# Cross-attention scores computed head by head in sixteen 32x32 places of the array, in plain fp32

## The reference, cut to what matters

```python
Q, K, V = x@Wq.T + bq, ctx@Wk.T + bk, ctx@Wv.T + bv      # 16 heads of 32
scores = einsum('bhqd,bhkd->bhqk', Q, K) / sqrt(32)
scores = where(scores <= softplus(raw_thresholds), -1e9, scores)
x = x + (softmax(scores) @ V -> 512) @ Wo.T + bo         # Q from layernorm(x)
```

## Time and profile before

| | |
|---|---|
| median of 3 runs | 1723.44 us |
| the profiled execution's own time | 1722.73 us |
| its span, first to last instruction | 1720.9 us |
| PE / PEld busy | 96% / 82% |
| DVE / ACT / POOL busy | 63% / 49% / 27% |
| granted TensorE clock, mean | 0.987 of full speed |

### The profile page before, as it was taken

One profiled execution on the slowest core, in us unless ns is written; L12 is line 12 of the kernel. 1 busy time (PEld: TensorE's weight loads), 2 busy tenths in 40 slices (PEclk: granted clock), 3 DMA queues, 4 the chain that ended last, 5 costly groups with the idle time before them and its releaser, 6 DMA issues.

```text
span 1720.9 us, 29176 instructions
## 1 busy us (share of the span) xinstructions
PE 1649.3 (96%) x10832; PEld 1402.7 (82%) x10832; DVE 1087.0 (63%) x2138; ACT 851.2 (49%) x1195; POOL 471.8 (27%) x357
## 2 busy tenths in 40 slices
PE   7999999999998899999998999999989999999997
PEld 6888889889887688788887887887877888888886
DVE  6554454554556767653337676635457989999995
ACT  4444444344444333344335233534416787878873
POOL 1443443444343344300004443300021121211311
PEclk9999999999999899999999999999999999999999
DMA  5011101110111300023224001224342443626612
GB/s 195 26 38 39 37 24 37 37 37 24 61 49 48 113 1 1 25 86 98 91 93 142 1 1 35 88 88 146 133 163 71 172 159 93 246 74 244 215 48 67
DMA packets 35977, 144.00 MB, mean 84 GB/s; under 512 B 4992, under 2 KB 5504, under 8 KB 28672
## 3 DMA queue, kind: packets, MB, share of 16 engines
q1 hardware_dynamic: 30736, 130.98, 21.7%
q0 software_dynamic: 5168, 12.06, 3.5%
HBM read 222.72 MB, written 12.85 MB: 137 GB/s over the span
## 4 chain that ended last, share of the span: by engine, by line
PE 56%; DVE 6%; DMA 2%; issue 1%; ACT 1%; SPq 0%; POOL 0%; DVEq 0%; POOLq 0%; ACTq 0%
PE bank L88 35%; PE bank L1608 9%; PE bank L2083 7%; PE bank L1505 2%; PE bank L2089 2%; PE bank L1592 1%; DVE e_w L2010 1%; DVE rc L1253 1%; DVE rs L1253 1%; DMA A<-xh_d,token 1%; DMA out<-acc_d 0%; PE bank L1517 0%; PE bank L1627 0%; DVE r_xh L1230 0%; DVE r_wg L1239 0%
## 5 line engine op out<-in xcount | busy, mean ns | idle before, releaser
L2010 DVE TENSOR_TENSOR e_w<-e_raw,e_w 128x2048 fp32r<-128x2048 f32 x134 | 302.4, 2284 | 20.3 <-ACT e_w L1892 19.8
L1892 ACT ACTIVATE e_w<-e_raw 128x2048 fp32r<-128x2048 f32 x134 | 256.6, 1918 | 38.4 <-PE bank L2083 19.2
L88 PE MATMUL bank<-e_w,e_xT 128*128 128x512 f32 x1104 | 272.1, 396 | 0.0
L88 PEld LDWEIGHTS bank<-e_w,e_xT 128*128 128x128 f32 x1104 | 204.3, 188 | 42.5
L88 PE MATMUL bank<-wv,ctx 128*128 128x512 f32 x768 | 190.8, 397 | 6.9 <-DVE kT L669 6.9
L88 PE MATMUL bank<-ctx,wk 128*128 128x258 f32 x1536 | 193.3, 285 | 2.1 <-issue 2.1
L88 PE MATMUL bank<-x2T,fw 128*128 128x512 f32 x768 | 190.4, 398 | 4.7 <-DVE fw L1314 4.7
L88 PEld LDWEIGHTS bank<-ctx,wk 128*128 128x128 f32 x1536 | 186.9, 190 | 4.0 <-issue 2.9
L1608 PE MATMUL bank<-fw,hh 128*128 128x512 f32 x768 | 186.1, 391 | 2.7 <-DVE hh L1432 2.7
L88 PEld LDWEIGHTS bank<-x2T,fw 128*128 128x128 f32 x768 | 145.2, 191 | 35.9 <-issue 5.0
L1608 PEld LDWEIGHTS bank<-fw,hh 128*128 128x128 f32 x768 | 143.9, 188 | 34.6 <-issue 2.2
(11 more groups left out here) (253 smaller groups left out, 2674.4 us busy)
## 6 DMA issues: line engine op xcount, KB each, us to landing
e_raw<-in_we SPq DMA_DIRECT2D x138, 1024.0 KB, 5.6
fraw<-in_wf SPq DMA_DIRECT2D x64, 512.0 KB, 3.5
ctxraw<-in_ctx SPq DMA_DIRECT2D x32, 514.0 KB, 3.5
wraw<-in_wa SPq DMA_DIRECT2D x20, 512.0 KB, 4.4
X<-in_x SPq DMA_DIRECT2D x4, 512.0 KB, 7.0
acc_d<-X SPq DMA_DIRECT2D x8, 256.0 KB, 4.5
xh_d<-A SPq DMA_DIRECT2D x8, 256.0 KB, 3.7
out<-acc_d SPq DMA_DIRECT2D x4, 512.0 KB, 5.9
```

What stands on the lines that cost most here:

```text
L88: last = nc.tensor.matmul(out, lhs(t, a), rhs(t, b), start=start and n == 0, stop=n == len(steps) - 1)
L1892: nc.scalar.activation(w[pos][:, 0, :, :], raw[pos][:, :, :], ACT.Copy).then_inc(m["w_hi"], 1)
L2010: nc.vector.tensor_tensor(w[pos][:, 1, :, :], raw[pos][:, :, :], r(w[pos][:, 0, :, :]), ALU.subtract).then_inc(m["w_lo"], 1)
```

## The change

- Queries and keys stay plain fp32: qT and kT have one half, the low halves of queries (eight VectorE instructions) and keys (four a batch) go, and the later steps wait for ScalarE's copy (`q_ok`, `k_ok`). GpSimd copies the batch's queries into qb (128 x 128) in place of qbd (128 x 1024).
- `score` becomes 16 plain fp32 products of 32 rows by 32 columns: head group g takes rows 32g to 32g+31, chunk c takes columns 32c to 32c+31, and the four g write four banks (4, 5, 2, 3). It stands as one piece ahead of the second half of V, and what it waits for is asked for before the last three products of the first half.
- All four thresholds follow each other; `turn(b-1)` stands behind the second half of V (and behind `project`); `attend` comes one batch later, between the second and third chunk of K, for batch b-2. `heads`, `bias_heads`, `project_lo` and `add_x` move with it: `add_x` from the body of k = 1 to the head of the body of k = 2.
- ScalarE copies both halves of V before `turned(b-1)`. In batch 31 it does the exponentials ahead of `turned(30)`; there `attend(30)` is done after the loop.
- The last row's product has plast as weights and the identity as moving operand; the constants own_q and same_head go, a block of ones comes.

TensorE in the third batch of the first tile: before, the scores stand in two pieces and `attend` at the end.

```diff
 S_BANK = (4, 5, 2, 3)
-        qT = sb("qT", [P, 2, DC, TOK], F32R)
+        qT = sb("qT", [P, DC, TOK])
-            kT = sbi("kT", [P, 2, DC, SKE], F32R)
+            kT = sbi("kT", [P, DC, SK])
@@ gpsimd
-                    def spread_q(b):
+                    def own_queries(b):
+                        nc.gpsimd.tensor_tensor(qb[:, :, :], qT[:, :, bass.ds(b * S, S)], ones[:, :].unsqueeze(1).broadcast_to([P, DC, S]),
+                                                ALU.mult).then_inc(qb_ok, 1)
@@ scalar
-                                nc.scalar.activation(kT[:, 0, dc, :], bank[K_BANK[dc]][:, 0:SKE], ACT.Identity, bias=col("bk", dc)).then_inc(k_hi, 1)
-                                if dc == 1 and k == 1 and not first:
+                                nc.scalar.activation(kT[:, dc, :], bank[K_BANK[dc]][:, 0:SK], ACT.Identity, bias=col("bk", dc)).then_inc(k_ok, 1)
+                                if dc == 3 and k == 1 and not first:
                                     heads_hi(it - 1)
...
-                            if not begin:
-                                turned(b - 1)
                             act.wait_ge(v_ps, 2 * b + 2)
                             nc.scalar.activation(v[k % 2][:, 1, :], bank[1][:, :], ACT.Copy).then_inc(v_ok, 1)
-                            exps(b)
+                            if last and k == BPT - 1:
+                                exps(b)
+                                turned(b - 1)
+                            else:
+                                if not begin:
+                                    turned(b - 1)
+                                exps(b)
@@ vector
-                            for dc in range(DC):
-                                dve.wait_ge(k_hi, DC * b + dc + 1)
-                                nc.vector.scalar_tensor_tensor(kT[:, 1, dc, :], ...
+                            if k == 2 and not first:
+                                add_x(it - 1)
+                            if not (first and k < 2):
+                                heads((k - 2) % BPT, b - 2)
                             if k == 1 and not first:
-                                add_x(it - 1)
+                                bias_heads(it - 1)
+                                project_lo(it - 1)
...
+                            threshold(b)
+                            softmax_terms(b)
...
                             weigh(b)
                             reciprocal(b)
-                            if not begin:
-                                heads((k - 1) % BPT, b - 1)
-                            if k == 0 and not first:
-                                bias_heads(it - 1)
@@ tensor
-                    def score(b, cs, begin):
...
+                    def score_waits(b, begin):
+                        pe.wait_ge(k_ok, DC * b + DC)
+                        pe.wait_ge(qb_ok, b + 1)
+                        if not begin:
+                            pe.wait_ge(u_ok, DC * b)
+                    def score():
+                        for g in range(HPC):
+                            rows = slice(g * XD, (g + 1) * XD)
+                            for c in range(DC):
+                                last = nc.tensor.matmul(bank[S_BANK[g]][c * S:(c + 1) * S, 0:SK], qb[rows, c, :], kT[rows, c, :], start=True, stop=True)
+                        last.then_inc(s_ps, 1)
...
+                                if dc == 1 and not (first and k < 2):
+                                    if not (first and k == 2):
+                                        pe.wait_ge(oT_ok, b - 2)
+                                    attend((k - 2) % BPT, b - 2, it if k == 2 and not first else None)
+                            pe.wait_ge(k_ok, DC * b + 1)
+                            for c in range(DC):
+                                if c == DC - 1:
+                                    score_waits(b, begin)
...
+                            score()
+                            pe.wait_ge(k_ok, DC * b + 2)
+                            products(nc, bank[1][:, :], range(DC), lambda c, h: ctx[k % 2][:, h, c, P:2 * P],
+                                     lambda c, h: wv[:, h, c, :]).then_inc(v_ps, 1)
                             if k == 1 and not first:
                                 project(it - 1)
                             if not begin:
-                                pe.wait_ge(k_lo, DC * b + DC)
                                 turn(b - 1)
-                            score(b, (0, 1), begin)
-                            value(1)
-                            score(b, (2, 3), begin)
```

More of the change, by code:

```diff
@@ L42 @@
 K_BANK = (0, 1, 4, 5)
+S_BANK = (4, 5, 2, 3)
 LATE_AT = 4
@@ L776, in turn @@
                         pe.wait_ge(plast_ok, b + 1)
-                        nc.tensor.matmul(bank[6][:, 0:P], same_head[:, :], plast[:, :, :].rearrange("p c n -> p (c n)"),
+                        if not (isinstance(b, int) and b == 0):
+                            pe.wait_ge(olast_ok, b)
+                        nc.tensor.matmul(bank[6][:, 0:P], plast[:, :, :].rearrange("p g n -> p (g n)"), ident[:, :],
                                          start=True, stop=True).then_inc(spread_ps, 1)
@@ L820, in body @@
                                          lambda c, h: ctx[k % 2][:, h, c, :]).then_inc(k_ps, 1)
-                            def value(kt):
-                                pe.wait_ge(k_lo, DC * b + 1 + kt)
-                                products(nc, bank[kt][:, :], range(DC), lambda c, h: ctx[k % 2][:, h, c, kt * P:(kt + 1) * P],
-                                         lambda c, h: wv[:, h, c, :]).then_inc(v_ps, 1)
-                            value(0)
+                                if dc == 1 and first and k == 1:
+                                    pe.wait_ge(u_ok, 2)
+                                if dc == 1 and not (first and k < 2):
[6 more added lines that the diff above has]
+                                    score_waits(b, begin)
+                                for n, (i, j) in enumerate(PARTS):
+                                    last = nc.tensor.matmul(bank[0][:, :], ctx[k % 2][:, i, c, 0:P], wv[:, j, c, :],
+                                                            start=c == 0 and n == 0, stop=c == DC - 1 and n == len(PARTS) - 1)
+                            last.then_inc(v_ps, 1)
+                            score()
+                            pe.wait_ge(k_ok, DC * b + 2)
+                            products(nc, bank[1][:, :], range(DC), lambda c, h: ctx[k % 2][:, h, c, P:2 * P],
+                                     lambda c, h: wv[:, h, c, :]).then_inc(v_ps, 1)
                             if k == 1 and not first:
@@ L829, in body @@
                             if not begin:
-                                pe.wait_ge(k_lo, DC * b + DC)
                                 turn(b - 1)
-                            score(b, (0, 1), begin)
-                            value(1)
-                            score(b, (2, 3), begin)
-                            if not begin:
-                                if not (first and k == 1):
-                                    pe.wait_ge(oT_ok, b - 1)
-                                attend(k - 1, b - 1, it if k == 1 and not first else None)
                     body(0, True)
@@ L841, in _ @@
                         body(it, False)
-                    turn(NB - 1)
+                    pe.wait_ge(oT_ok, NB - 2)
+                    attend(BPT - 2, NB - 2, None)
+                    turn(NB - 1, False)
                     pe.wait_ge(e["xh"], 1)
```

101 lines of the change are left out of this document (34 added, 67 removed).

## The result

The changed kernel takes 1698.3 us, the median of 4 runs (1696.3 to 1702.93); the kernel before, run beside it, 1723.95 (1722.08 to 1725.44). The ratio is 0.9856, with a 95% interval from 0.9833 to 0.9878. The profiled execution took 1697.46 us, its span is 1695.7.

A forecast was written before the change was run, and what follows sets the result against it. TensorE was taken to bound the kernel, busy 414.0 of 420 us in the cross-attention. The terms -23.4 - 4.5 - 4.0 + 7.7 - 1.3 = -25.5 us took 1722.7 to 1697.2, a median of 1698, range 1688 to 1706.

The forecast's parts named there:

- Scores: Cross-attention scores on TensorE: sixteen packed products take 0.89 us a batch instead of 1.62, a gain of 23.4 us.
- what goes is 1.62: The two old score pieces on TensorE, 0.80 + 0.82 us a batch from start to start, disappear.
- a packed stage has its entry and exit wherever it stands: TensorE's transposes, packed products and `project` are only moved, so they cost nothing between their neighbours.
- under 0.75 means that the stream runs at fp32r's pace: Profile sign for the scores' group of 32 records, forecast at about 0.9 us from its start to V's.
- Waits that go: V no longer waits for VectorE's low half of the keys: 4.5 us gained, and 4.0 in the first batch.
- The wait that comes: At k = 2 `attend` on TensorE waits for VectorE's `add_x`, 1.1 us in seven tiles: 7.7 us lost.
- What stays covered: The scores' wait for GpSimd's copy of the queries stays hidden, with 1.7 us of slack.
- The end: TensorE's idle time ahead of the last transposes falls from 5.64 to 4.4 us, a gain of 1.3.
- The range: Whole kernel: 1688 to 1706 us, from the ends of the stream, the new wait (0 to 10 us) and the end.
- Two row groups at once: Rival for the scores: two row groups run together, not four, 1.28 us a batch, total 1710 us; chance 0.13.
- turns: Rival for the scores: places sharing rows run one after another, 2.17 us a batch, total 1739 us; chance 0.08.
- the softmax chain: Rival: the chain ends later than counted and the scores wait for the queries; at 3 us, 1738 us; chance 0.05.

The follow-up runs named there:

- the joined: Changed kernel with `attend` moved from the middle of K to right ahead of the scores for k = 0, 2 and 3: 1687.56 us, again 1685.34 us.
- split `attend`: Changed kernel with `add_x` put back into k = 1 ahead of `last_token`, and `attend` in two halves between the first three chunks of K: 1697.01 us.
- The early `add_x`: Changed kernel with `add_x` put back into the body of k = 1, now ahead of `last_token`: 1687.76 us, again 1688.86 us.
- the other order of places: Changed kernel with the sixteen score products reordered, chunks outside and row groups inside: 1699.72 us.
- four whole-array plain products: Changed kernel with the scores as four plain fp32 products on the whole array in place of sixteen packed ones: 1727.07 us.
- the two faster versions: Changed kernel with `add_x` ahead of `last_token` in k = 1, and changed kernel with `attend` right ahead of the scores; side by side 1688.86 and 1685.34 us.

## Why the prediction was right, step by step

The mechanism was right, and the total too, 1698 for 1698.3, but by terms that erred to both sides. That they meet within 0.3 us is luck: the batches gained 3.2 us less than counted, 2.1 us came from idle time that I had overlooked, and the clock took 1.5 us ahead of the first batch and gave 1.2 behind the last.

- **Scores, mis-sized.** What comes was 0.84 us for 0.89. The starts took 0.10, not 0.14, and two records 2 x 0.21, close to the 0.46; the row that I took for the stream, the plain product on the whole array, was the right one. What failed is "what goes is 1.62". Twelve products at K's pace of 0.123 are 1.48. The other 0.14 was the price of switching between whole-array and packed or plain products, and it did not go: `attend` now stands inside K, and K takes 6.05 us for 5.91. That is what the joined and the split `attend` measured: 0.17 less for a switch less, 0.28 more for one more. So "a packed stage has its entry and exit wherever it stands" was right for the neighbours, and the same cost was counted in the scores as a gain. A batch gained 0.63 instead of 0.73 (its period is 14.20 us for 14.1), 32 x 0.63 = 20.2 us instead of 23.4. The sign "under 0.75 means that the stream runs at fp32r's pace" was wrong too: the stage shows 0.64 at 0.21 a record, because 0.20 of the 0.84 us shows in the halves of V.
- **Waits that go:** as read, 4.5 us and the first batch 4.2 for 4.0. Missed: K's idle time behind `attend`, 2.1 us in all, which lies in the same view as the others.
- **The wait that comes:** 7.8 us for 7.7, at the place named. The early `add_x` shows that it is all VectorE's order.
- **The long stretch** of 19.9 us is 31 x 0.63 = 19.5, the 1.0 that changed sides, 4.5 and 2.1 gained and 7.8 lost, together 19.3; 0.6 has no row.
- **What stays covered:** the queries' copy ends at 334.24, and the scores ask 9/12 through the first half of V, at 334.65 + 9/12 x 2.89 = 336.82. The slack is 2.6 us for 1.7, and no wait of the scores on GpSimd appears.
- **The end:** the idle time ahead of the last transposes fell from 5.64 to 2.56 + 1.13 = 3.7 us, not to 4.4. The products of the retention behind it ran 2.4 us shorter (3.06 for 5.49), and 1.4 of that was lost again to VectorE's r_xh (6.81 for 5.38). Predicted 1.1, measured 2.4: up to the last transposes 1.2 were gained, about what I counted (1.95 of idle time, less 0.77 in the pieces beside it). The 1.2 behind them are not the change's: the products of the retention ran at a granted clock of 0.50 before (559.39 to 565 us) and of 1.00 after (535.57 to 538.5 us).
- **The start** lost 1.5 us. The granted clock from 12 to 20 us was 0.71 after and 0.79 before, from 20 to 32 us 0.91 and 1.00. The experiments' first K begins between 43.1 and 47.0 us with that stage unedited, so this is no part of the change.
- **The range.** With the new wait at its own lower end of 0 us and the other two ends beside it the sum reaches 1681, not 1688; the upper end, 1706, is added up rightly.
- **Rivals.** Two row groups at once and turns are refuted by the stage of 0.84 us with entry and exit, where they asked for 1.28 and 2.17, by the sixteen starts in 0.10 us and by the other order of places; the softmax chain by the empty waits. The figure of the Trainium skill that the prediction cites ("TensorE: Matmul & The Clock Gate", Part 3, "Measured speedup vs the span model"), 4 ns a place, is nearer to the measured 6.7 than my 9, and both are off by less than 0.05 us a batch.

## What to carry to other kernels

When a stage is replaced, price what goes by the pace of its own instructions, not from start to start: the switch into and out of a neighbour of another shape stays and turns up beside that neighbour. Small products that fill all places of the array are worth it by their stream alone (0.64 us for what four whole-array plain products do in 1.55), and are best kept to one stage of no more than 32 records, beside another packed one (0.17 us a batch in the trace; the medians of the two faster versions don't decide it). Look at where the freed banks and moved steps stand on the engine off the path: `add_x` moved by one softmax on VectorE cost TensorE 7.8 us.

## What the runs showed of the hardware

- Sixteen 32 x 32 places run together in either order that was tried, with starts 6.7 ns apart.
- A plain fp32 record streams a column in 0.82 ns on 32 x 32 places (0.21 us less for two records of 128 columns fewer). On the whole array its records of 257 columns start 0.216 us apart, 0.84 ns a column.
- In a packed stage of 64 records of 257 columns the second 32 take 0.66 us to start, the first 0.34; a stage of 32 behind one of 64 of another width is not slowed. What sets this is open.
- The stretch ahead of the first batch was up to 3.9 us longer in one kernel than in another that differs only behind it; where it is longest, twelve query products take 5.46 us, as they do at a recorded clock of 0.50.
- VectorE's `bias_heads` (128 x 512, L619 before) takes 2.30 us beside GpSimd and 0.69 us at 559.6 us, where GpSimd is idle.
